# One-hot tiles transposed by DMA instead of by TensorE and ScalarE, in a two-layer vision block

## The reference

```python
# layer 0 (alpha = 1, beta = 0)
y = einsum('nchw,dc->ndhw', gn(x), Wp) + bp          # 512 channels
# split into 8 heads (fc) and 2 x 2 regions of 64 x 64 pixels: m = n*fc*4 clusterings
x_point, x_value = 32 + 32 channels of each pixel     # centres: 8 x 8 block means, s = 64
sim   = sigmoid(alpha * cos(x_point, c_point) + beta) # (m, 4096, 64)
max_v, max_i = sim.max(2), sim.argmax(2)
agg   = concat(c_value, 1).at[max_i].add(max_v * concat(x_value, 1)); agg = agg[:-1] / agg[-1]
disp  = max_v * agg[max_i]
x     = x + einsum('nchw,dc->ndhw', disp, Wm) + bm
# layer 1
s = sigmoid(w2 @ relu(w1 @ (diagonal DCT average of gn(x))))
out = x + gn(x) * s
```

## Time and profile before

| | |
|---|---|
| median of 3 runs | 5098.84 us (5097.33 to 5101.37) |
| profiled execution, its own time | 5106.24 us |
| its span, first to last instruction | 5104.5 us |
| mean granted TensorE clock | 0.978 |
| busy: PE / DVE / ACT / POOL | 94% / 80% / 72% / 62% of the span |
| DMA | 665 MB, 130 GB/s |

### The profile page before, as it was taken

One profiled execution on the slowest core, in us unless ns is written; L12 is line 12 of the kernel. 1 busy time (PEld: TensorE's weight loads), 2 busy tenths in 40 slices (PEclk: granted clock), 3 DMA queues, 4 the chain that ended last, 5 costly groups with the idle time before them and its releaser, 6 DMA issues.

```text
span 5104.5 us, 154703 instructions
## 1 busy us (share of the span) xinstructions
PE 4784.7 (94%) x59984; PEld 4697.0 (92%) x59984; DVE 4082.1 (80%) x8662; ACT 3687.3 (72%) x8683; POOL 3185.3 (62%) x3423
## 2 busy tenths in 40 slices
PE   1999999999999999999999999999999999999950
PEld 1899999999999999999999999999999999999940
DVE  3788888888888888888888888888888878887730
ACT  4877777777777777777777777777777777767621
POOL 1455665666666676666766666766766667666640
PEclk9999999999999999999999999999999999999975
DMA  5333233455555455554555555554555444444238
GB/s 165 84 88 101 81 90 89 123 140 136 148 148 148 129 148 148 148 144 131 148 147 146 139 138 147 145 147 134 145 147 145 135 111 116 117 115 117 80 104 201
DMA packets 1295754, 665.33 MB, mean 130 GB/s; under 512 B 1105952, under 2 KB 1106352, under 8 KB 1295024
## 3 DMA queue, kind: packets, MB, share of 16 engines
q1 hardware_dynamic: 1295024, 655.43, 47.3%
HBM read 395.15 MB, written 260.05 MB: 128 GB/s over the span
## 4 chain that ended last, share of the span: by engine, by line
PE 91%; DMA 2%; ACT 2%; SPq 2%; issue 1%; DVE 1%; POOL 1%; POOLq 0%; ACTq 0%
PE bank L1013 58%; PE bank L1093 9%; PE bank L1115 7%; PE bank L1176 7%; PE bank L1155 5%; PE bank L1147 4%; SPq L342 1%; DMA chunk<-x 1%; DMA out<-fin 1%; DVE pool L866 0%; ACT ysq L800 0%; PE bank L1041 0%; ACT chunk L650 0%; PE bank L1048 0%; DVE gath L914 0%
## 5 line engine op out<-in xcount | busy, mean ns | idle before, releaser
L616 POOL TENSOR_TENSOR xl<-xr,xh 128x512 fp32r<-128x512 f32 x512 | 653.9, 1277 | 1316.9 <-ACT xh L813 1308.0
L787 ACT ACTIVATE yh<-bank,bpf 128x256 fp32r<-128x256 f32 x1024 | 429.4, 471 | 543.6 <-PE bank L1013 542.3
L909 DVE TENSOR_REDUCE rank<-bank 128x8 f32<-128x512 f32 x1024 | 705.3, 691 | 46.8 <-PE bank L1013 13.8
L631 POOL TENSOR_TENSOR vals<-vals,vpart 128x528 f32<-128x528 f32 x512 | 613.9, 1199 | 144.0 <-ACT vpart L823 142.4
L635 POOL TENSOR_TENSOR dl<-dsq,dh 128x512 fp32r<-128x512 f32 x512 | 661.5, 1292 | 63.5 <-ACT dsq L819 63.5
L925 DVE TENSOR_TENSOR hot<-bank,rank 128x512 bf16<-128x512 f32 x1024 | 652.9, 676 | 0.0
L578 POOL TENSOR_TENSOR vpart<-vals,vpart 128x528 bf16<-128x528 f32 x512 | 616.0, 1203 | 40.5 <-ACT vpart L757 38.8
L1013 PE MATMUL bank<-xh,wph 128*128 128x256 f32 x2048 | 619.0, 302 | 13.4 <-POOL xl L616 13.4
L1013 PE MATMUL bank<-dh,wmh 128*128 128x256 f32 x2048 | 625.1, 305 | 3.6 <-POOL dl L635 3.6
L1013 PE MATMUL bank<-ch,yh 128*128 128x256 f32 x2048 | 622.8, 304 | 0.0
L959 DVE SCALAR_TENSOR_TENSOR yl<-bank,bpf,yh 128x256 fp32r<-128x256 f32 x1024 | 448.1, 479 | 199.7 <-ACT ysq L800 199.6
(11 more groups left out here) (170 smaller groups left out, 14644.9 us busy)
## 6 DMA issues: line engine op xcount, KB each, us to landing
chunk<-x SPq DMA_DIRECT2D x512, 256.0 KB, 3.4
xr<-x SPq DMA_DIRECT2D x1024, 128.0 KB, 3.3
mixed<-xr SPq DMA_DIRECT2D x480, 256.0 KB, 2.0
fin<-mixed SPq DMA_DIRECT2D x480, 256.0 KB, 3.1
out<-fin SPq DMA_DIRECT2D x960, 128.0 KB, 3.0
out<-xr SPq DMA_DIRECT2D x64, 128.0 KB, 2.8
wraw<-wp_t SPq DMA_DIRECT2D x1, 512.0 KB, 4.1
ws<-wm_t SPq DMA_DIRECT2D x1, 256.0 KB, 2.8
```

The lines of the kernel that those rows point to most:

```text
L616: pool.tensor_tensor(xl[:, G0 % 2], xr[:, G0 % SLOTS], xh[:, G0 % 2].bitcast(F32), ALU.subtract).then_inc(s_xl, 1)
L631: pool.tensor_tensor(vals[:, G2 % 2], vals[:, G2 % 2], vpart[:, 0], ALU.subtract).then_inc(s_r1, 1)
L787: op = nc.scalar.activation(yh[:, m], y_ps[:, m], ACT.Identity, bias=b[:, m:m + 1])
L909: op = V.tensor_reduce(rank[:, t], sims[t], axis=AX.X, op=ALU.max)
```

## The change

The 8 TensorE transposes and ScalarE's copy go. SyncE issues, at the head of its step i, two DMA transposes for group G3 = i-3, each from `hot[:, G3 % 2, t]`, [128 pixels, 512], to `hot_t[:, G3 % HOTS, :, t*128:(t+1)*128]`, [128, 4, 128], both in SBUF. It first waits for the gather that used the slot (`s_g`), for the transposes four groups back (`s_te[G % 4]`, 4 semaphores, 32 counts a group) and for the one-hot of the tile. VectorE now waits, before it overwrites a slot of `hot`, for the transposes of the group that used it. TensorE's gather waits for `s_te` of its group; its other waits for `s_te` and for the readers of bank 4 ahead of the transposes go.

```diff
--- before.py
+++ after.py
@@ -192,7 +192,6 @@
         n_ps = bank[0]
         s_ps = [bank[1], bank[2]]
         v_ps = bank[3][:, :].rearrange("p (t h c) -> p t h c", t=TILES, h=HEADS)
-        t_ps = bank[4][:, :].bitcast(BF16).rearrange("p (k f) -> p k f", k=KT)
         a_ps = bank[5][:, 0:KT * AGG].rearrange("p (k c) -> p k c", k=KT)
         g_ps = bank[6]
         d_ps = bank[6][:, :].rearrange("p (m f) -> p m f", m=M)
@@ -225,8 +224,7 @@
         s_z = sem("argument")
         s_ez = sem("exponential")
         s_mv = sem("similarity")
-        s_t = sem("transposed")
-        s_te = sem("transposed_kept")
+        s_te = sems("transposed", 4)
         s_v1 = sem("values_part1")
         s_r1 = sem("values_rest1")
         s_v2 = sem("values_part2")
@@ -290,9 +288,6 @@
                     at = gate_links.index(link)
                     order["gate", n, at], step_of["gate", n, at] = len(order) + 1, i
 
-        def used_until(i):
-            return max(order[use] for use in order if step_of[use] <= i)
-
         @block.sync
         def _(sp):
             for dst, src in ((bp_s, bp_col), (bm_s, bm_col), (alpha_s, alpha), (beta_s, beta), (s0_s, first_centre),
@@ -324,6 +319,14 @@
                 sp.wait_ge(s_tmp[J % 4], upto(J // 4 - 1, 16))
                 sp.dma_start(tmp[J], xr[:, J % SLOTS].rearrange("p k f -> p (k f)")).then_inc(s_tmp[J % 4], 16)
 
+            def transpose_hot(G):
+                sp.wait_ge(s_g, upto(G - HOTS))
+                sp.wait_ge(s_te[G % 4], upto(G // 4 - 1, 16 * TILES))
+                for t in range(TILES):
+                    sp.wait_ge(s_hot[t], upto(G))
+                    sp.dma_start_transpose(hot_t[:, G % HOTS, :, t * P:(t + 1) * P], hot[:, G % 2, t]
+                                           ).then_inc(s_te[G % 4], 16)
+
             def band_groups(n, b):
                 fh, g = b // GROUPS, b % GROUPS
                 first = n * PER + fh * 2 * GROUPS + g
@@ -350,6 +353,8 @@
                 load_chunk(u)
 
             for i in range(STEPS):
+                if on(i - 3):
+                    transpose_hot(i - 3)
                 if AHEAD <= i + AHEAD < NG:
                     load_x(i + AHEAD)
                 if on(i - ADD) and i - ADD < NG - 2 * GROUPS:
@@ -799,10 +804,6 @@
                     for m in range(M):
                         op = nc.scalar.activation(ysq[:, m], y_ps[:, m], ACT.Square, bias=b[:, m:m + 1])
                     op.then_inc(s_sq, 1)
-                if on(G3):
-                    act.wait_ge(s_t, upto(G3))
-                    act.wait_ge(s_g, upto(G3 - HOTS))
-                    nc.scalar.activation(hot_t[:, G3 % HOTS], t_ps, ACT.Copy).then_inc(s_te, 1)
                 if i % PER == 1 and PER < i < NG:
                     act.wait_ge(s_v, upto(i - 2))
                     weights_high(i // PER, 1)
@@ -921,6 +922,8 @@
                     V.tensor_tensor(zarg[:, G2 % 2], rank[:, :, :].rearrange("p t h -> p (t h)"), rnorm[:, G2 % 2],
                                     ALU.mult).then_inc(s_z, 1)
                     dve.wait_ge(s_agg, upto(G2 - 2))
+                    if G2 >= 2:
+                        dve.wait_ge(s_te[(G2 - 2) % 4], upto((G2 - 2) // 4, 16 * TILES))
                     for t in range(TILES):
                         V.tensor_tensor(hot[:, G2 % 2, t].rearrange("p (h s) -> p h s", h=HEADS), sims[t],
                                         rank[:, t].rearrange("p (h o) -> p h o", o=1).broadcast_to(
@@ -1076,12 +1079,10 @@
                 G1, G2, G3, J1, J2 = i - 1, i - 2, i - 3, i - GATHER, i - MIX
                 for n, link in fold_at(i):
                     if link in fold_links:
-                        pe.wait_ge(s_te, upto(min(G3, NG) - 1))
                         clear("fold", n, fold_links.index(link))
                         fold(n, fold_links.index(link))
                 for n, link in gate_at(i):
                     if link in gate_links:
-                        pe.wait_ge(s_te, upto(min(G3, NG) - 1))
                         clear("gate", n, gate_links.index(link))
                         gate(n, gate_links.index(link))
                 if on(G2):
@@ -1104,7 +1105,7 @@
                                        [((yh[:, m, px], yl[:, m, px]), (ch[:, R % 2, m], cl[:, R % 2, m]))])
                         op.then_inc(s_sim[t], 1)
                 if on(J1):
-                    pe.wait_ge(s_te, upto(J1))
+                    pe.wait_ge(s_te[J1 % 4], upto(J1 // 4, 16 * TILES))
                     pe.wait_ge(s_dh, upto(J1 - 1))
                     if J1 % GROUPS == 0:
                         pe.wait_ge(s_tab, upto(J1 // GROUPS))
@@ -1138,15 +1139,6 @@
                                    [((xh[:, b, k, px], xl[:, b, k, px]),
                                      (wph[:, k, C:2 * C], wpl[:, k, C:2 * C])) for k in range(K)])
                     op.then_inc(s_v, 1)
-                if on(G3):
-                    pe.wait_ge(s_te, upto(G3 - 1))
-                    pe.wait_ge(s_fr, used_until(i))
-                    for t in range(TILES):
-                        pe.wait_ge(s_hot[t], upto(G3))
-                        for kt in range(KT):
-                            op = nc.tensor.transpose(t_ps[:, kt, t * P:(t + 1) * P],
-                                                     hot[:, G3 % 2, t, kt * P:(kt + 1) * P], identb[:, :])
-                    op.then_inc(s_t, 1)
                 if on(J1):
                     pe.wait_ge(s_d, upto(J1))
                     for m in range(M):
```

## The result

The changed kernel takes 4885.98 us (median of 4 runs, 4881.53 to 4887.91), the kernel before 5100.1 us on the same chip: ratio 0.9579, 95% interval 0.9563 to 0.9596, so 4.2% faster. 4895 us was predicted. The profiled execution took 4887.86 us with a span of 4886.0 us: 218.5 us less than the span before.

The account below looks back on a forecast made before the run. TensorE was taken to bound nearly every step. From the profiled 5106.24 us, minus 210 for the transposes, plus 5 allowance, gave 4901; the median lying 7.4 lower gave 4894, stated as 4895 us (own range 4870 to 4930).

Parts of the forecast that it names:

- The bound, and that nothing takes its place: TensorE bounds nearly every step, 9.13 us; at 8.72 us VectorE still fits, its norms wait shrinking from 0.49 to 0.08.
- 512 x 0.41 = 210 us: TensorE's order: eight transposes removed save 0.41 us a step by weight-load starts, over 512 steps 210 us.
- 5 us of allowance: VectorE ends last in 32 steps at 0.16 us, from a region's statistics once in 16 steps: 5 us lost in all.
- a delay of 2 to 4 us is within those leads: SyncE's queue: x loads, stores, bands and chunks behind its new wait are issued two to four steps ahead, tolerating 2-4 us.
- ScalarE's 1.02 us a step worth nothing: ScalarE, 72% busy, already waits at VectorE and TensorE; removing its 1.02 us copy a group gains nothing by itself.
- Cost of the DMA transposes: nothing: SyncE's queue and DMA engines: the pair takes 0.9 us to issue with 4.95 us free a step, so hidden.
- The cover in time: From SyncE's issue to VectorE's overwrite of `hot`: 10.2 us after the change for the pair, which takes 6.8 one after the other.
- rival A: SyncE's queue bounds each step, DMA transposes one after the other at 3.5 us each: about 5850 us, chance 0.25.
- the 256-byte estimate: DMA engines: transposes moving in 256-byte rows make 1024 packets a step, 64 an engine, 1.9 us, hidden.
- Rival B: DMA engines full, transposes cut into very small pieces, 20.1 us a step: about 10700 us, chance 0.08.
- Rival C: DMA transposes hidden, but VectorE takes back half of the gain: about 4995 us, chance 0.09.
- D: Break-even: the pair lands just at 10.2 us and waits eat the gain: within 0.2% of before, 5099 us, chance 0.03.

Follow-up runs that it names:

- experiment 3: Kernel before, TensorE transposes kept, no DMA transposes; ScalarE copies only 16 of 1024 columns from the 19th group on: 5098.34 us, ratio 0.9998.
- experiment 4: Changed kernel with the chunk loads moved to the head of SyncE's step, ahead of the transposes and their wait for the gather: 4877.17 us, ratio 0.9565.
- Experiments 1: Changed kernel with DMA transposes of the first 18 groups only, the other 494 groups' left out and not replaced: 4875.54 us, ratio 0.9562.

## Why the prediction was right

*The bound, and that nothing takes its place.* Right. TensorE is 999.18 us of 1000 busy, and of VectorE's three waits the one for the norms shrank: 0.49 us before, while the changed kernel's L901 at 2503.76 follows on its predecessor. The other two waits, which I said would give way if needed, are there in the same step:

```profile
2503.76 0.16 DVE L901 TENSOR_SCALAR rnorm<-bank 128x16 f32<-128x16 f32 x1
...
2508.66 0.25 DVE L955 RECIPROCAL mv<-ez 128x16 f32<-128x16 f32 x1 [0.23 <-ACT ez L800]
...
2509.39 0.88 DVE L962 SCALAR_TENSOR_TENSOR yl<-bank,bpf,yh 128x256 fp32r<-128x256 f32 x2 [0.36 <-ACT ysq L805]
```

One step is a thin base, so here are the sums from 1500 to 2500 us (us, times, longest), of the kernel before and of the changed one:

```profile
DVE rnorm L900 <- PE bank L1093: 58.3, 94, 2.6
...
DVE mv L952 <- ACT ez L795: 45.9, 97, 1.3
DVE yl L959 <- ACT ysq L800: 38.5, 106, 0.5
```

```profile
DVE mv L955 <- ACT ez L800: 71.1, 108, 2.6
...
DVE yl L962 <- ACT ysq L805: 39.5, 110, 0.4
DVE rnorm L901 <- PE bank L1094: 13.3, 17, 2.1
```

The wait for the norms falls to 13.3 us, about 0.12 a step, as forecast. The wait for ScalarE at L955 grows instead of giving way.

*512 x 0.41 = 210 us.* The term was undersized: 0.466 us a step over 511 steps is 238 us. I had taken the distance between the starts of two weight loads. The matmuls of the same two lines start 0.45 us apart (2504.32 and 2504.77), and that was the price to read. The bubble that I saw ahead of the weight loads (they start 0.11 us after the last value matmul starts) was no bubble for the matmuls: L1147 started 0.12 us after the last value matmul before the change, and the L1147 of the changed kernel does the same. The waits that went with the transposes can't be much of the gain: in mid-run the weight load ahead of them idled 2.0 us in all before the change.

*5 us of allowance.* Undersized as well, and in another place than I had put it. It is not the region's statistics. By the table in the result, at 0.466 us a step, 7.9 us are missing in the 17 steps from group 0 to 17, 10.9 in the rest of the first image and 2.0 ahead of group 0, and 1.3 come back at the end: 19.5 us instead of 5. For the steps without a gather the sum had no term: it gave TensorE's saving to all 512 steps, while these 17 are not TensorE's. TensorE's granted clock between 142 and 275 us is 0.95, against 0.97 before and 0.99 in experiment 3, where these 17 steps take 124.6 us; its part is not separated. The 2.0 us ahead of group 0 may be chance: experiment 4 reaches it at 127.07 us. The first image is a step of the working that failed: "a delay of 2 to 4 us is within those leads". It held for x and the bands and not for the chunks of the first image. The working took them to be loaded two steps ahead; there they are loaded 0 or 1 step ahead, and those with 0 waited. Experiments 1 and 4 show it from both sides.

That 4895 us came within 9 us is in part luck. The gain was 28 us too small and the losses 14.5 us too small, which cancel to 13: the working's 4901 us stands against 4887.86 us for the profiled execution. And the median lies only 1.9 us under the profiled execution, not 7.4, which takes another 5.5 us off the difference.

*ScalarE's 1.02 us a step worth nothing.* Right (experiment 3).

*Cost of the DMA transposes: nothing.* Right in its result in mid-run and wrong in its size. I took 0.9 us of SyncE for the pair, near the plain issues; it is 2.5 us. The rows themselves should have warned me: I read 0.34 to 0.48 us an issue from them, but four stores there take 2.28 us and two loads of x 1.91 us, up to 0.96 us each. It stayed hidden since 2.5 us is still below the 4.95 us which the working gave as the room. With four a step, 5.0 us, the room is used up, and SyncE sets the step. The cover in time held too: the second transpose of the pair starts about 1.4 us after the first and lands 2.5 us later, so the pair is done in about 4 of the 10.2 us. So rival A's place and its deciding point were right, its price (3.5 us each, one landing after the other) was not: issues follow each other while earlier ones are still under way. For the DMA engines, packets rose as the 256-byte estimate had it (544 and not 512 a DMA), and their time from 0.473 x 5104.5 to 0.661 x 4886.0 us of 16 engines: 815 us for 1024, 0.80 us each, 1.6 a step against 1.9 estimated. Rival B falls with that. Rival C (VectorE takes back half) falls with the 8.67 us step, and D with it.

The Trainium skill's 1309 ns for 128 x 128 in bf16 by DMA ("VectorE: DVE Perf Modes", section "The three transpose paths") is near the 1232 ns for which each of the eight holds SyncE. The page doesn't say what its time spans; from issue to landing each of the eight takes 2.4 us. It is in any case no price of a tile: 128 x 1024 holds SyncE for 1239 ns.

The Trainium skill ("Advanced Engine Details and Errata", section "X-Bar Transpose (TRN2)") has transposes as fast as regular DMAs, at 350 to 400 GB/s. No run here shows such a rate: 131 KB in 0.80 us of 16 engines is about 165 GB/s, where the plain DMAs before moved 655.43 MB in 0.473 x 5104.5 = 2414 us of 16 engines, 271 GB/s. But these two compare packets of different sizes. The plain DMAs' packets of 2048 bytes take 102.9 ns of an engine (318 GB/s on 16) and those of 256 bytes 17.85 ns (229 GB/s). With eight transposes a step, when the queue is emptiest, the mean over all 256-byte packets, a third of them transposed, is 17.99 ns; in the changed kernel it is 19.29 ns. So for packets of one size the trace with eight agrees that transposes are about as fast. What makes the packets longer in the changed kernel, the transposes or the fuller queue, is not separated.

## What to carry to other kernels

Work that a full engine does for layout alone can go to the DMA queues, and its worth is the distance from its first start to the next operation's first start on that engine (0.45 us here), times the steps that this engine really bounds (not those at the start, here). Price the move at the queue that issues it: here a DMA transpose holds SyncE about 1.24 us from 128x128 to 128x1024, so make each as large as its data allow, and count the issues of a step against the step, by their mean and with the gaps between them. Then see what stands behind them on that queue: count each load's lead in steps phase by phase. Here the chunk loads had a lead of 1 or 2 steps in most of the run and were on time; in the first image some had none, and these came late.

## What the runs showed that I had not expected

- The issue time of a DMA transpose does not depend on its size: 1232 ns for 128x128, 1246 for 128x256, 1258 for 128x512, 1239 for 128x1024 (medians). Plain DMAs took 0.43 to 0.59 us each in the step shown of the kernel with four. From issue to landing 128x512 took 2.5 us, 128x1024 3.1.
- Each carries 32 packets of 4 bytes beyond its 256-byte rows: 544 for 512 rows, and (1835696 - 1295024) / 512 = 1056 for 1024 rows.
- The same 256 KB a step in two pieces gives a 4.2% faster kernel than before, in four a 4.9% slower one.
